# Cross attention's probabilities turned two steps behind, its last tiles added while it drains, and the query weight's low half made in parts on VectorE

## The chip, the cores and the metric

The kernel runs on one core of a Trainium2 chip. The metric is the device time of one execution in microseconds (us). A core has five engines that work beside each other and meet only in semaphores: TensorE (PE in the profile; PEld is its loading of weights), VectorE (DVE), ScalarE (ACT), GpSimd (POOL) and SyncE (SP), which here only issues transfers from device memory. Each engine takes its instructions strictly in the order in which they are written: an instruction that waits holds up all that stand behind it on its engine.

## What is computed

One block of a transformer on 32 sequences of 32 tokens, 512 wide, all in float32:

```python
x = x + xattn(layernorm(x), ctx, ctx)   # 16 heads of 32; ctx is (32, 257, 512)
x = x + attn(layernorm(x))              # self attention, four projections 512x512
x = x + ffn(layernorm(x))               # shared SwiGLU + 64 experts, top 8, 1536 wide

def xattn(q, k, v):                     # heads split from the 512 columns, no projections
    scores = einsum('bhqd,bhkd->bhqk', q, k) / sqrt(32)
    return einsum('bhqk,bhkd->bhqd', softmax(scores), v)
```

## The kernel before

The program has four stages, one behind the other, each a block in which the five engines run their own lists: cross attention (tiles named `a_...`, to about 201 us), self attention (`b_...`, to 353 us), the router with the shared network (`d_...`, to about 600 us) and the 64 experts (`e_...`, the rest). The 1024 tokens lie in eight tiles X of 128 x 512. Each of the first three stages begins with a layer norm of all eight tiles on VectorE (`layernorm`, line 81), with one square root on ScalarE in it.

**Cross attention** goes over 32 batches of 32 queries and 257 keys. A step of the loop does, for batch b:

- `scores(b)` on TensorE (line 250): four matmuls, one for four heads each, into PSUM banks 0 to 3. The queries of four heads stand as a block diagonal in `Q` (128 x 128), which GpSimd copies from XT (line 235). Before it, TensorE waits for K of batch b (`k_in`) and for the exponentials of batch b-1, which read the same banks.
- the largest score of each row on VectorE (`largest`, lines 336 and 340, in two halves), the exponential on ScalarE (line 316) into `PR`, and the division by the sum on VectorE (`normalise`, lines 346 and 348).
- `turn` on TensorE (lines 262 and 263): the normalised PR is transposed into banks 4 to 6. ScalarE copies two parts of it to `PTa` (line 310), VectorE the third to `PTb` (line 356).
- `values` on TensorE (line 281): 48 small matmuls with V into bank 7, which `place_out` on VectorE (line 329) copies to `AT`.

TensorE's list of step b is scores(b), values(b-3), turn(b-1). K and V have four buffers each. SyncE's list, which issues all of their copies, is

```python
for b in range(B):
    i = b % 4
    if b >= 4:
        sp.wait_ge(s_done, 2 * (b - 3))
    sp.dma_start(K[:, i, :, :], ctx_k[b])            # line 206
    if b >= 4:
        sp.wait_ge(pv_done, b - 3)
    sp.dma_start(V[0:KC, i, 0:2, :], ...)            # line 209
    sp.dma_start(V[0:KR, i, 2, :], ...)              # line 210
```

Here `s_done` counts finished halves of scores and `pv_done` finished `values`. V of batch b therefore waits for values(b-4), which frees its buffer, and K of batch b+1 stands behind V of batch b in the same list. After the last V come the four projection weights `W` of the next stage.

Once the loop has ended, the eight tiles of AT are transposed back (line 298), added to X (line 367), and the sums for the next layer norm are taken (`tile_stats`, line 76).

**Self attention** splits each float32 operand into a high half (ScalarE) and a low half, the remainder (VectorE), and multiplies three times. Its start: layer norm of eight tiles; ScalarE makes the high half of the query weight (line 567); GpSimd makes its low half (line 436) and clears `PT` (line 437); TensorE transposes four tiles in two banks (line 447), ScalarE copies them (line 591), VectorE finds masked tokens (line 622) and makes the low halves (line 624); then TensorE projects queries and keys of the first four tiles (lines 453 to 455), transposes the other four, and projects those. ScalarE takes the queries (line 581), VectorE the keys (line 637).

**The router's stage** begins in the same way, and GpSimd fills the masks and number tables for it (lines 1111 to 1119) as soon as the stage begins.

Of the kernel before, what the change touches and what calls it, by code (L numbers as in the profile page):

```python
# [10 lines left out]
ALU = mybir.AluOpType  # L11
# [69 lines left out]
def layernorm(dve, X, XN, mv, small, done, std_ready, xn_ready):  # L81
# [9 lines left out]
    for t in range(TT):  # L91
        dve.tensor_scalar(XN[:, t, :], X[:, t, :], mv[:, t, 0:1], r[:, t:t + 1],
                          ALU.subtract, ALU.mult).then_inc(xn_ready, 1)
# [22 lines left out]
def program(nc, x, ctx_k, ctx_v, wq, wk, wv, wo, bq, bk, bv, bo, wg, shared, experts, out):  # L116
    root = ExitStack()
    with root:
# [19 lines left out]
        narrow = sb("narrow", [1, NE], I32)  # L138
        x_dram = x.rearrange("b s d -> (b s) d").rearrange("(t p) d -> p t d", p=P)
# [11 lines left out]
        with ExitStack() as st:  # L151
# [3 lines left out]
            Q = sb("a_Q", [P, 4, G, P])  # L155
            K = sb("a_K", [P, 4, G, SK])
            V = sb("a_V", [P, 4, 3, D])
            PR = sb("a_PR", [P, 2, G, SK])
# [19 lines left out]
            zeroed = sem("a_zeroed")  # L178
            ident_ready = sem("a_ident_ready")
            q_ready = sem("a_q_ready")  # L180
# [12 lines left out]
            x1_ready = sem("a_x1_ready")  # L193

# [24 lines left out]
            def _(pool):  # L219
                pool.memset(ident[:, :], 0.0).then_inc(made, 1)  # L220
                pool.memset(Q[:, :, :, :], 0.0).then_inc(zeroed, 1)
# [3 lines left out]
                pool.wait_ge(zeroed, 1)  # L225

                for b in range(B):
                    i = b % 4
                    if i == 0:
                        pool.wait_ge(xt_copied, b // 4 + 1)  # L230
                    if b >= 4:
                        pool.wait_ge(s_done, 2 * (b - 3))
                    for h in range(4):
                        r = slice(32 * h, 32 * h + 32)
                        pool.tensor_copy(Q[r, i, :, r], XT[r, :, SQ * b:SQ * (b + 1)]).then_inc(q_ready, 1)

            @block.tensor
            def _(pe):
# [3 lines left out]

                def scores(b):
                    i = b % 4
                    pe.wait_ge(q_ready, 4 * b + 4)
                    pe.wait_ge(k_in[i], 16 * (b // 4) + 16)
                    for g in range(G):
                        if b >= 1:
                            pe.wait_ge(exp_done, 4 * (b - 1) + g + 1)
                        last = pe.matmul(ps[:, g, 0:SK], Q[:, i, g, :], K[:, i, g, :], start=True, stop=True)  # L250
                        if g % 2 == 1:
                            last.then_inc(s_done, 1)

                def turn(b):
# [5 lines left out]
                    for g in range(G):  # L260
                        for k in range(2):
                            pe.transpose(ps[0:KC, 4 + k, g * P:(g + 1) * P], PR[:, b % 2, g, k * KC:(k + 1) * KC], ident[:, :])
# [1452 lines left out]
```

## Time and profile before

| | |
|---|---|
| time, median of 3 runs | 2543.09 us (2541.92 to 2548.95) |
| the profiled execution: its time, its span | 2544.21 us, 2542.5 us |
| cross attention, to the end of its last sums | 200.9 us |
| self attention | 201.4 to 352.9 us |
| TensorE busy over the span | 2435.0 us (96%) |
| busy in one step of cross attention of 4.80 us | PE 4.27, DVE 3.91, ACT 3.00, POOL 2.04 us |

How to read it: the span runs from the first to the last instruction of the one profiled execution; its time is 1.7 us longer. From about 600 us on TensorE is busy practically all the time, and the change touches nothing there. What the change can move lies in the first 400 us, where the engines wait for each other. The granted clock of TensorE is written as a share of 2.4 GHz, so that 0.50 is 1.2 GHz.

### The profile page before, as it was taken

The numbers are of one execution on the slowest core, as the hardware profiler recorded it, in microseconds if no ns is written. First come the engines' busy times: TensorE is split into PE (matmuls) and PEld (weight loads), VectorE is DVE, ScalarE is ACT, GpSimd is POOL, SyncE is SP. The second block draws the span as 40 slices with busy tenths as digits, with TensorE's granted clock in tenths as the row PEclk, the third lists the DMA queues.
The fourth block names the chain that finished last, engine by engine and source line by source line (L and its number), as shares of the span: only waits on it lengthen the run. The fifth ranks groups of instructions, "written<-read, shape, count | busy, mean of one in ns | idle before, by whom it ended". The sixth has DMA issues, their size and how long they took to land.

```text
span 2542.5 us, 53551 instructions
## 1 busy us (share of the span) xinstructions
PE 2435.0 (96%) x22042; PEld 1994.8 (78%) x22042; DVE 1995.0 (78%) x1896; ACT 1690.0 (66%) x2119; POOL 639.5 (25%) x542
## 2 busy tenths in 40 slices
PE   6876989998999999999999999999999999999998
PEld 5765767776888888888888888888888888888886
DVE  6866557665799889998978988988778777767795
ACT  5642333334688778887867887877667767766784
POOL 3411010001132332332222233223222222222221
PEclk9987989998999999999999999999999999999999
DMA  6870022244899999998979999999888888887894
GB/s 201 224 221 0 2 106 110 86 161 166 300 378 381 362 344 384 375 374 332 375 288 326 367 355 351 385 356 344 303 296 325 327 300 325 326 296 280 311 372 133
DMA packets 128526, 714.99 MB, mean 281 GB/s; under 512 B 15488, under 2 KB 23808, under 8 KB 52416
## 3 DMA queue, kind: packets, MB, share of 16 engines
q1 hardware_dynamic: 102048, 665.96, 67.9%
q0 software_dynamic: 26144, 44.06, 8.3%
q8 instruction: 273, 4.47, 0.7%
q14 instruction: 61, 0.50, 0.1%
HBM read 684.46 MB, written 25.49 MB: 279 GB/s over the span
## 4 chain that ended last, share of the span: by engine, by line
PE 75%; issue 0%; DVE 0%; POOL 0%; ACT 0%; ACTq 0%; POOLq 0%; DVEq 0%
PE ps L1539 14%; PE ps L1541 14%; PE ps L1540 14%; PE ps L1617 7%; PE ps L1619 7%; PE ps L1618 7%; PE ps L1570 5%; PE ps L1589 4%; PE ps L1602 3%; PE ps L1527 1%; PE ps L1580 1%; PE ps L1530 0%; DVE e_WL L1430 0%; ACT e_WH L1348 0%; POOL out_rows L1501 0%
## 5 line engine op out<-in xcount | busy, mean ns | idle before, releaser
L1430 DVE TENSOR_TENSOR e_WL<-ring,e_WH 128x2048 fp32r<-128x2048 f32 x462 | 1057.3, 2289 | 234.0 <-ACT e_WH L1348 228.7
L1348 ACT ACTIVATE e_WH<-ring 128x2048 fp32r<-128x2048 f32 x462 | 885.1, 1916 | 125.1 <-PE ps L1541 56.9
L1539 PE MATMUL ps<-e_WH,e_XEh 128*128 128x512 f32 x1536 | 605.1, 394 | 3.6 <-DVE e_XEl L1452 3.6
L1541 PE MATMUL ps<-e_WH,e_XEl 128*128 128x512 f32 x1536 | 599.4, 390 | 0.0
L1540 PE MATMUL ps<-e_WL,e_XEh 128*128 128x512 f32 x1536 | 598.8, 390 | 0.0
L1489 POOL TENSOR_TENSOR e_tick<-e_tick 128x1 f32<-128x1 f32 x126 | 111.9, 888 | 1305.2 <-ACT X L1396 1184.6
L1539 PEld LDWEIGHTS ps<-e_WH,e_XEh 128*128 128x128 f32 x1536 | 289.0, 188 | 62.0 <-DVE e_XEl L1452 4.0
L1541 PEld LDWEIGHTS ps<-e_WH,e_XEl 128*128 128x128 f32 x1536 | 288.9, 188 | 61.2
L1540 PEld LDWEIGHTS ps<-e_WL,e_XEh 128*128 128x128 f32 x1536 | 289.1, 188 | 58.0
L1617 PE MATMUL ps<-e_WH,e_GTh 128*128 128x512 f32 x768 | 318.8, 415 | 0.0
L1430 DVE TENSOR_TENSOR e_WL<-e_more,e_WH 128x2048 fp32r<-128x2048 f32 x114 | 260.8, 2289 | 53.8 <-ACT e_WH L1348 52.5
L1619 PE MATMUL ps<-e_WH,e_GTl 128*128 128x512 f32 x768 | 301.7, 393 | 0.0
L1618 PE MATMUL ps<-e_WL,e_GTh 128*128 128x512 f32 x768 | 299.3, 390 | 1.1 <-issue 1.1
L1348 ACT ACTIVATE e_WH<-e_more 128x2048 fp32r<-128x2048 f32 x114 | 218.5, 1916 | 27.5 <-PE ps L1541 14.3
L1503 POOL DMA_INDIRECT out_rows<-X,lists x64 | 174.4, 2726 | 19.5 <-issue 19.5
L1619 PEld LDWEIGHTS ps<-e_WH,e_GTl 128*128 128x128 f32 x768 | 144.1, 188 | 33.9
L1618 PEld LDWEIGHTS ps<-e_WL,e_GTh 128*128 128x128 f32 x768 | 145.1, 189 | 26.4 <-issue 1.4
L1617 PEld LDWEIGHTS ps<-e_WH,e_GTh 128*128 128x128 f32 x768 | 144.5, 188 | 23.8 <-issue 0.4
L1356 ACT ACTIVATE X<-ps 128x512 f32<-128x512 f32 x192 | 115.3, 601 | 62.8 <-PE ps L1541 62.8
L1438 DVE TENSOR_TENSOR X<-X,ps 128x512 f32<-128x512 f32 x192 | 130.6, 680 | 4.0 <-PE ps L1541 4.0
L744 POOL DMA_INDIRECT XO<-xn_scratch,lists x64 | 127.1, 1986 | 19.5 <-issue 18.6
L1458 DVE TENSOR_TENSOR e_GTl<-ps,e_GTh 128x512 fp32r<-128x512 f32 x192 | 131.1, 683 | 0.0
(224 smaller groups left out, 3314.6 us busy)
## 6 DMA issues: line engine op xcount, KB each, us to landing
ring<-in_experts SPq DMA_DIRECT2D x462, 1024.0 KB, 8.3
e_more<-in_experts SPq DMA_DIRECT2D x114, 1024.0 KB, 8.4
ring<-in_shared SPq DMA_DIRECT2D x12, 1536.0 KB, 6.5
a_K<-in_ctx_k SPq DMA_DIRECT2D x32, 514.0 KB, 5.4
a_V<-in_ctx_v SPq DMA_DIRECT2D x32, 384.0 KB
a_V<-in_ctx_v SPq DMA_DIRECT2D x32, 130.0 KB
X<-in_x SPq DMA_DIRECT2D x4, 512.0 KB, 4.9
xn_scratch<-ring SPq DMA_DIRECT2D x1, 2048.0 KB, 7.4
```

What stands on the lines that cost most here:

```text
L1348: act.activation(WH[:, nth % HELD, :], unit(i), ACT.Copy).then_inc(hi_done, 1)
L1430: dve.tensor_tensor(WL[:, at, :], unit(place(kind, n)), WH[:, at, :], ALU.subtract).then_inc(lo_done, 1)
L1438: dve.tensor_tensor(GF[n % 2], SL[n % 2], up_ps, ALU.mult).then_inc(gf_done, 1)
L1458: dve.tensor_tensor(GTl[:, n % 2, :, :], turn_ps.rearrange("p (j n) -> p j n", j=G), GTh[:, n % 2, :, :], ALU.subtract).then_inc(gtl_done, 1)
L1503: pool.indirect_dma_start(out4, bass.IndirectOffsetOnAxis(lists[:, 1, e, 1:2], 0), Y2, None, compute_op=ALU.add).then_inc(added, 16)
L1539: pe.matmul(dst, h, wh, start=(k == 0), stop=False)
L1540: pe.matmul(dst, h, wl, start=False, stop=False)
L1541: last = pe.matmul(dst, l, wh, start=False, stop=(k == G - 1))
L1570: pe.matmul(over_ps[32 * c:32 * c + 32, kind * P:(kind + 1) * P], XEo[:, e % 2, k, :], w[:, k * D + c * P:k * D + (c + 1) * P], start=(kin ...
L1617: pe.matmul(down_ps, h, wh, start=(b == 0 and j == 0), stop=False)
L1618: pe.matmul(down_ps, h, wl, start=False, stop=False)
L1619: last = pe.matmul(down_ps, l, wh, start=False, stop=(b == NB - 1 and j == G - 1))
```

## The change

Five parts.

1. *Scores without the block diagonal.* `Q` and GpSimd's copies are gone. `scores` multiplies the 32 rows of each head from XT with K, four matmuls of 32 x 32 x 257 for each of four groups; the result of head h of group g lands in output rows 32*((g+h) mod 4), and `values` reads it from there.
2. *Turned two steps behind.* TensorE's step is now scores(b), values(b-4), turn(b-2). PR has three buffers. ScalarE and VectorE copy the turned parts three steps behind, and VectorE does both halves of `largest` before `normalise`. SyncE's list is unchanged.
3. *The last tiles are added in the drain.* Each of the steps 32 to 35 also transposes two tiles back, adds them and takes their sums.
4. *GpSimd idle during layer norms.* In self attention the clearing of PT waits until the first queries are taken; in the router's stage the masks and tables wait until all eight normalised tiles are written. After the last work of ScalarE in the first two stages, a square root into an unused tile is added, which leaves the table for square roots loaded.
5. *Start of self attention.* The query weight's low half is made in four column parts on VectorE, the first behind four tiles of the layer norm, the others behind the other four. Four PSUM banks instead of two hold transposed tiles, and the masks of four tiles are found by one instruction. TensorE transposes tiles 4 to 7 between the query and the key projection of the first half.

The core of the diff:

```diff
@@ scores, on TensorE @@
-                        last = pe.matmul(ps[:, g, 0:SK], Q[:, i, g, :], K[:, i, g, :], start=True, stop=True)
+                        for h in range(4):
+                            r = slice(32 * h, 32 * h + 32)
+                            last = pe.matmul(ps[column(g, h), g, 0:SK], XT[r, g, at], K[r, i, g, :], start=True, stop=True,
+                                             skip_group_check=True)
@@ the loop on TensorE @@
-                for b in range(B + 3):
+                for b in range(B + 4):
                     if b < B:
                         scores(b)
-                    if b >= 3:
-                        values(b - 3)
-                    if 1 <= b <= B:
-                        turn(b - 1)
+                    if b >= 4:
+                        values(b - 4)
+                    if 2 <= b <= B + 1:
+                        turn(b - 2)
+                    for t in tiles_back(b):
+                        turn_back(t)
@@ the loop on VectorE @@
+                for b in range(B + 4):
+                    if 3 <= b < B + 3:
+                        copy_rest(b - 3)
                     if b < B:
                         largest(b, 0)
+                        largest(b, 1)
                     if 1 <= b <= B:
                         normalise(b - 1)
-                    if b < B:
-                        largest(b, 1)
-                    if b >= 3:
-                        place_out(b - 3)
+                    if b >= 4:
+                        place_out(b - 4)
+                    for t in tiles_back(b):
+                        add_attended(t)
@@ self attention, GpSimd @@
-                pool.wait_ge(wh_done, 1)
-                pool.tensor_tensor(pair(QUERY)[1], whole(QUERY), pair(QUERY)[0], ALU.subtract).then_inc(wl_pool, 1)
+                pool.wait_ge(q_copied, 1)
                 pool.memset(PT[:, :, :, :, :], 0.0).then_inc(zeroed, 1)
@@ end of ScalarE's list in cross attention; the same in self attention @@
+                act.activation(unused[:, :], ident[:, 0:1], ACT.Sqrt)
@@ router's stage, GpSimd @@
+                pool.wait_ge(xn_ready, TT)
                 pool.memset(before[:, :], 1.0).then_inc(masks, 1)
```

**TensorE, one step in the middle of cross attention.** `a_k_in0` is the arrival of K in buffer 0, `a_v_in1` that of V in buffer 1, and so on; the order of the kernel before:

```order
L250 MATMUL ps<-a_K,a_Q 128x257 [waits a_exp_done,a_k_in0,a_q_ready]
L250 MATMUL ps<-a_K,a_Q 128x257 [waits a_exp_done] x3
L281 MATMUL ps<-a_PTa,a_V 32x32 [waits a_v_in1,a_at_ready,a_ptb_ready,a_pta_ready]
L281 MATMUL ps<-a_PTa,a_V 32x32 x7
L281 MATMUL ps<-a_PTb,a_V 32x32 x4
...
L262 MATMUL ps<-ident,a_PR 96x128 [waits a_ptb_ready,a_pta_ready,a_pr_ready]
L262 MATMUL ps<-ident,a_PR 96x128
```

and of the changed kernel:

```order
L253 MATMUL ps<-a_K,a_XT 32x257 [waits a_exp_done,a_k_in1]
L253 MATMUL ps<-a_K,a_XT 32x257 x3
L253 MATMUL ps<-a_K,a_XT 32x257 [waits a_exp_done]
...
L286 MATMUL ps<-a_PTa,a_V 32x32 [waits a_v_in1,a_at_ready,a_ptb_ready,a_pta_ready]
L286 MATMUL ps<-a_PTa,a_V 32x32 x7
L286 MATMUL ps<-a_PTb,a_V 32x32 x4
...
L266 MATMUL ps<-ident,a_PR 96x128 [waits a_ptb_ready,a_pta_ready,a_pr_ready]
L266 MATMUL ps<-ident,a_PR 96x128
```

The wait for GpSimd's copies (`a_q_ready`) is gone, scores are sixteen matmuls, and the values that stand behind the scores of buffer n are now those of buffer n itself (the batch four steps back) and no longer those of buffer n+1.

**VectorE, the end of cross attention**, from the last division of scores on, before (of eight additions two are shown):

```order
L348 TENSOR_TENSOR a_PR<-a_PR,a_rs 128x1028
L329 COPY a_AT<-ps 128x4x32
L356 COPY a_PTb<-ps 65x512
L329 COPY a_AT<-ps 128x4x32 x2
L367 TENSOR_TENSOR X<-X,ps 128x512
L76 BN_STATS stats<-X 128x6
L78 BN_AGGR mv<-stats 128x2
```

and now:

```order
L363 TENSOR_TENSOR a_PR<-a_PR,a_rs 128x1028
L344 COPY a_AT<-ps 128x4x32
L369 TENSOR_TENSOR X<-X,ps 128x512
L76 BN_STATS stats<-X 128x6
L78 BN_AGGR mv<-stats 128x2
...
L377 COPY a_PTb<-ps 65x512
L344 COPY a_AT<-ps 128x4x32
```

The additions stand between the copies of the last steps and no longer behind all of them.

**VectorE, the start of self attention**, before:

```order
L90 TENSOR_TENSOR small<-small 128x8
L92 TENSOR_SCALAR b_XN<-X,mv,small 128x512 x8
L622 TENSOR_SCALAR b_mask<-ps 1x128
L624 TENSOR_TENSOR b_XTl<-ps,b_XTh 128x512
...
L630 TENSOR_TENSOR b_WP<-W,b_WP 128x2048
L679 TENSOR_TENSOR X<-X,bvo 128x512 x8
L637 TENSOR_SCALAR b_KT<-ps,bqk 128x512 x4
```

and now:

```order
L97 TENSOR_TENSOR small<-small 128x8
L84 TENSOR_SCALAR b_XN<-X,mv,small 128x512 x4
L659 TENSOR_TENSOR b_WP<-W,b_WP 128x4x128
L647 TENSOR_TENSOR b_XTl<-ps,b_XTh 128x512 x4
L652 TENSOR_SCALAR b_mask<-ps 1x512
L84 TENSOR_SCALAR b_XN<-X,mv,small 128x512 x4
L659 TENSOR_TENSOR b_WP<-W,b_WP 128x4x128 x3
L664 TENSOR_TENSOR b_WP<-W,b_WP 128x2048
L718 TENSOR_TENSOR X<-X,bvo 128x512 x8
```

Half of the layer norm has moved behind what the first projection waits for, and the quarter of the query weight's low half that it needs first has moved ahead of the transposed tokens.

## Rows read from the trace of the kernel before

**Rows 1.** Windows: length; busy time (instructions) of each engine; PEclk; DMA share; GB/s.

```profile
35.60:35.90 0.30, 0.30 (x40) 0.23 (x26) 0.30 (x1) 0.30 (x2) 0.30 (x1) 1.00 0.00 0
...
100.00:104.80 4.80, 4.27 (x118) 3.56 (x117) 3.91 (x8) 3.00 (x11) 2.04 (x4) 1.00 0.85 218
...
175.00:180.00 5.00, 4.22 (x109) 3.75 (x112) 0.78 (x2) 0.49 (x1) 0.00 (x0) 0.52 1.01 406
```

**Rows 2.** Timeline, PE, one step: start, length, line, names, count [idle before].

```profile
99.94 1.91 PE L250 MATMUL ps<-a_K,a_Q 128*128 128x257 f32 x8
101.78 0.33 PE L281 MATMUL ps<-a_PTa,a_V 96*32 96x32 f32 x16
...
103.33 0.42 PE L262 MATMUL ps<-ident,a_PR 128*96 128x128 f32 x2 [0.53 <-DVE a_PR L348]
...
104.58 0.27 PE L263 MATMUL ps<-ident,a_PR 128*65 128x128 f32 x1
```

**Rows 3.** Timeline, SyncE, in the same step: issue of V.

```profile
102.84 0.31 SPq L209 DMA_DIRECT2D a_V<-in_ctx_v  x1
```

**Rows 4.** Timeline: issue of a later K on SyncE, and the scores that use it.

```profile
127.82 1.44 SPq L206 DMA_DIRECT2D a_K<-in_ctx_k  x1
...
133.96 1.98 PE L250 MATMUL ps<-a_K,a_Q 128*128 128x257 f32 x8 [0.17 <-issue]
```

**Rows 5.** DMA issues, landing in us: the K issued at 127.82, then that at 36.80.

```profile
a_K<-in_ctx_k SPq DMA_DIRECT2D x1, 514.0 KB, 6.1
...
a_K<-in_ctx_k SPq DMA_DIRECT2D x1, 514.0 KB, 5.5
```

**Rows 6.** Tile a_K, all 32 copies: time from issue to landing.

```profile
DMA to landing us min/median/max: 3.5/5.4/13.7
```

**Rows 7.** Timeline, SyncE: V of batch 4, then K of batch 5.

```profile
35.97 0.31 SPq L209 DMA_DIRECT2D a_V<-in_ctx_v  x1
...
36.80 0.35 SPq L206 DMA_DIRECT2D a_K<-in_ctx_k  x1
```

**Rows 8.** Timeline, PE, in the drain: after a pause, and a whole turn.

```profile
175.78 0.27 PE L281 MATMUL ps<-a_PTb,a_V 65*32 65x32 f32 x3 [2.67 <-issue]
...
176.68 0.66 PE L262 MATMUL ps<-ident,a_PR 128*96 128x128 f32 x2
...
179.05 0.42 PE L263 MATMUL ps<-ident,a_PR 128*65 128x128 f32 x1
```

**Rows 9.** Timeline, PE, at the start of self attention's projections.

```profile
220.01 0.76 PE L453 MATMUL ps<-b_XTh,b_WP 128*128 128x512 f32 x1 [1.69 <-DVE b_XTl L624]
...
223.09 0.39 PE L454 MATMUL ps<-b_XTl,b_WP 128*128 128x512 f32 x1
```

**Rows 10.** Timeline: V of batch 31 on SyncE; VectorE's last sums of cross attention.

```profile
165.85 0.31 SPq L209 DMA_DIRECT2D a_V<-in_ctx_v  x1
...
200.74 0.18 DVE L78 BATCH_NORM_AGGREGATE mv<-stats 128x2 f32<-128x6 f32 x1
```

**Rows 11.** Timeline: eight tiles normalised (first, second layer norm); two of them turned, PE.

```profile
12.47 3.74 DVE L92 TENSOR_SCALAR a_XN<-X,mv,small 128x512 f32<-128x512 f32 x8
...
204.07 11.37 DVE L92 TENSOR_SCALAR b_XN<-X,mv,small 128x512 f32<-128x512 f32 x8
...
204.67 1.97 PE L447 MATMUL ps<-ident,b_XN 128*128 128x128 f32 x8 [6.55 <-DVE b_XN L92]
```

**Rows 12.** Timeline: last keys of the first half, first queries of the second.

```profile
243.51 0.75 DVE L637 TENSOR_SCALAR b_KT<-ps,bqk 128x512 f32<-128x512 f32 x1 [1.97 <-PE ps L455]
...
251.69 0.69 ACT L581 ACTIVATE b_QT<-ps,bqk 128x512 f32<-128x512 f32 x1 [4.04 <-PE ps L455]
```

**Rows 13.** Timeline, third layer norm: a 128x8 operation on VectorE; ScalarE behind a transfer.

```profile
355.13 4.17 DVE L89 TENSOR_SCALAR small<-small 128x8 f32<-128x8 f32 x1
...
360.27 1.06 ACT L890 ACTIVATE d_UPh<-ring 128x1024 fp32r<-128x1024 f32 x1 [5.88 <-DMA ring<-in_shared]
```

**Rows 14.** Timeline, PE, self attention: scores of one tile in 32 x 32 pieces.

```profile
319.88 1.29 PE L506 MATMUL ps<-b_KT,b_QT 32*32 32x32 f32 x128
```

More of the change, by code:

```diff
@@ L78, in tile_stats, with layernorm_tiles, layernorm @@
     dve.bn_aggr(mv[:, t, :], stats[:, t, :]).then_inc(stats_done, 1)
-def layernorm(dve, X, XN, mv, small, done, std_ready, xn_ready):
+def layernorm_tiles(dve, X, XN, mv, small, xn_ready, first, end):
+    for t in range(first, end):
+        dve.tensor_scalar(XN[:, t, :], X[:, t, :], mv[:, t, 0:1], small[:, 1, t:t + 1],
+                          ALU.subtract, ALU.mult).then_inc(xn_ready, 1)
+def layernorm(dve, X, XN, mv, small, done, std_ready, xn_ready, first=0, end=TT):
     var, r, a = small[:, 0, :], small[:, 1, :], small[:, 2, :]
@@ L90, in layernorm @@
     done.then(dve.tensor_tensor(r, r, a, ALU.mult))
-    for t in range(TT):
-        dve.tensor_scalar(XN[:, t, :], X[:, t, :], mv[:, t, 0:1], r[:, t:t + 1],
-                          ALU.subtract, ALU.mult).then_inc(xn_ready, 1)
+    layernorm_tiles(dve, X, XN, mv, small, xn_ready, first, end)
 def transpose_tiles(pe, ps, XN, ident, xn_ready, xt_psum, xt_copied):
@@ L543, in project_out @@
                     last.then_inc(o_psum, 1)
-                for half in range(2):
-                    for t in range(4 * half, 4 * half + 4):
-                        turn_tile(t)
-                    project(QUERY, half)
-                    project(KEY, half)
+                for t in range(4):
+                    turn_tile(t)
+                project(QUERY, 0)
+                for t in range(4, TT):
+                    turn_tile(t)
+                project(KEY, 0)
+                project(QUERY, 1)
+                project(KEY, 1)
                 for t in range(TT + 3):
@@ L672, in add_out @@
                     tile_stats(dve, X, stats, mv, t, o_added, t + 1, stats2)
-                layernorm(dve, X, XN, mv, small, Tally(dve, ln_done), std_ready, xn_ready)
+                layernorm(dve, X, XN, mv, small, Tally(dve, ln_done), std_ready, xn_ready, 0, 4)
+                query_weights_low(0)
                 for t in range(4):
                     tokens_low(t)
+                find_masked(0)
+                layernorm_tiles(dve, X, XN, mv, small, xn_ready, 4, TT)
+                for o in range(1, G):
+                    query_weights_low(o)
                 weights_low(KEY)
```

133 lines of the change are left out of this document (68 added, 65 removed).

## The prediction

> **What bounds the kernel now.** I read four views, in this order. The windows by stage show that the engines share the work only in the first 400 us, and that one step of cross attention lasts 4.80 us with TensorE busy for 4.27 and VectorE for 3.91 of it [rows 1]: no engine is full, so a chain through several engines or a transfer sets the step. The timeline of TensorE shows one such chain: scores at 99.94, values at 101.78, then 0.53 us of waiting for VectorE's division, the turn from 103.33 to 104.85, and the next scores at once [rows 2]. The change goes for this chain, and the 0.53 us are what it can win in a step.
>
> The timeline of SyncE together with the landings shows a second chain, just as long. V of a batch goes out the moment values(b-4) is done (102.84) [rows 3], and K of the next batch behind it. The K issued at 127.82 takes 6.1 us and lands at 133.92; its scores begin at 133.96, after TensorE has stood idle for 0.17 us, which the profile files under issue because it shows no transfer there [rows 4, 5]. So in the kernel before K is already only just in time, with a whole step plus a turn of lead.
>
> **Part by part. The queue that the values are moved past.** In the changed kernel values(b-4) is done in step b, not in step b-1. SyncE's list is as before: V(b) waits for it, and K(b+1) waits in the list behind V(b), though its own buffer has long been free. Step b+1 begins with scores(b+1), which need this K. Of the lead (a turn and a whole step) only the turn is left, 1.5 us [rows 2]. The loop is now closed within one step: K landed, scores, values, V issued, K issued, K landed. Its terms:
>
> - scores and values at full clock: from 99.94 to the issue of V at 102.84, 2.90 us [rows 2, 3].
> - from V's issue to K's landing: V of batch 4 goes out at 35.97 and K of batch 5 at 36.80, into a DMA queue that had nothing to do just before (share 0.00), which is how it will be in every step of the changed kernel. K lands 5.5 us later, 6.33 us after V's issue [rows 1, 5, 7]. In the worst place it was 0.83 + 6.1 = 6.9. A K of 3.5 us, the shortest of all 32, is the bound on the other side: 4.3 [rows 6]. I take 6.33, the case that is alike.
>
> That is a step of 9.23 us in place of 4.81 at full clock, with TensorE idle for 6.33 - 1.52 = 4.8 us in each.
>
> **The clock.** In the drain of the kernel before, TensorE paused for 2.67 us up to 175.78 and went on at a granted clock of 0.52, which is its lower level of 1.2 GHz [rows 1, 8]. A turn then took from 176.68 to 179.47, 2.79 us, against 1.52 at 2.4 GHz, a factor of 1.84 [rows 2, 8]. It came back to full clock 3.1 us after the projections had begun at 220.01 (a matmul of 512 columns goes from 0.76 to 0.39 us) [rows 9]. With a pause longer than 2.67 us in every step, each step's scores should begin at the low level. If scores and values all run there they take 2.90 x 1.84 = 5.34 us and the step 11.67; if the clock returns after 3.1 us, these do 1.7 us of the work and the remaining 1.2 us run at full clock: 4.3, and a step of 10.6. I take the middle, 11.1, since nothing in the rows decides it. The Trainium skill describes this very loop (TensorE: Matmul & The Clock Gate, "HAM oscillation"): matmuls, then a wait for a transfer, and every round starts throttled again; by it every step pays. The trace agrees for one pause, at 175.78; no run here shows a repeated one.
>
> **The scores themselves.** 16 matmuls of 32 x 32 in place of 4 of 128 x 128: each of the 8 passes of 257 columns takes about 0.23 us (1.91 / 8), and there are now 32 passes. If the four heads' pieces run at the same time the cost is nothing; if in pairs, 1.9 us more; if one by one, 5.5 more [rows 2]. In self attention 128 passes of 32 columns in such pieces take 1.29 us [rows 14]; one by one they would take 128 x 0.23 x 32/257 = 3.7. I take nothing. The Trainium skill (TensorEngine Tiling (Array Packing), "Gotcha 1: PSUM Pressure") speaks against this form: pieces in different row groups cannot write one PSUM bank at the same time, and here all four do. By that rule they would run one by one; the row at 319.88, also four row groups in one bank, is nearly three times faster than that, so I give the rule a small chance.
>
> The copies on GpSimd (2.04 us per step [rows 1]) cost nothing before and win nothing now.
>
> **Sum of the loop.** V(4) goes out after values(0), in step 4 instead of 3, but the steps before it are shorter, since their K is there: it stays near 36 (2 us either way). Then 27 steps of 11.1: V(31) at 335.7 in place of 165.85 [rows 10], **+169.8 us**.
>
> **The drain.** From V(31) to the end of the last sums it was 200.92 - 165.85 = 35.1 us [rows 10]. Now VectorE does the eight additions with their sums (1.52 us each, 12.2 in all: they fill 188.67 to 200.92 today) between the copies, and its own work in the four last steps, with one division and seven copies, comes to 18 us. Two waits for TensorE and pauses like the 2.67 us [rows 8] stay: I take 24, **-11** (from -14 to -5).
>
> **Start of self attention.** Eight tiles take 11.37 us while GpSimd works, and 3.74 while it doesn't, 0.47 each [rows 11]. The stage begins at 201.4. Its small operations take 2.65 us before the first tile at 204.07 and without the table load 1.3 less; so the first tile is there after 1.35 + 0.47 + some 0.3 of semaphores = 2.1 us. TensorE turns two tiles in 1.97 us at the low clock [rows 11], four in 4: 6.1. ScalarE's copy and VectorE's low half of the last one, 0.6 and 0.7, end at 7.5. VectorE meanwhile has four tiles (1.9) and a quarter of the weight (0.7) done. I put the first projection at 7.7 us; it was 18.6 (220.01) [rows 9]: **-10.9**. Between the halves: from the last keys (PE done near 243.5) to the second half's first queries at 251.69, less the 2.7 us that a group takes, lie 5.5 us [rows 12]; four tiles turned in a row at full clock cost 2: **-3.5**. GpSimd's clearing of PT now falls on the key weight's low half; that has 5 us of slack behind the second set of turns.
>
> **Third layer norm.** One operation on 128x8 elements took 4.17 us beside GpSimd [rows 13]; its neighbours of the same size take 0.17. Without that and the table load the layer norm is 5.4 us shorter. But ScalarE can copy nothing before 361.33, since it waits for the first weights, issued when the stage begins [rows 13]: the gain stops there, **-0.3**.
>
> Total: 169.8 - 11 - 10.9 - 3.5 - 0.3 = +144. The span becomes 2686.5 us, the profiled execution, 1.7 us longer than its span, 2688, and the median of the runs, 1.1 us under it, **2687 us**.
>
> **The rivals.**
> 1. *The clock holds.* The loop as above, but with 9.23 us in a step: 27 x 1.87 = 50 us less, and 2.5 less in the drain: 2634. For it: the work of a step is 4.4 us, longer than the 3.1 that brought the clock back. Against it: the pause.
> 2. *Scores in pairs or one by one.* In pairs +1.9 (3.5 at low clock) in each of 27 steps gives 2740 to 2780; one by one 2835 to 2960.
> 3. *Faster: K arrives in time.* If the copies no longer queue behind a backlog, the landing after V's issue could shrink. The step would fall to TensorE's 4.27 us [rows 1] only if K landed 1.5 us after V's issue; then 27 x 0.54 = 15, 11 and 15 us are won: 2502. All parts together break even where a step lasts 5.8 us, a landing 2.9 us after V's issue. The quickest case that the rows allow is 4.3, a step of 7.2 and 2579 us; that mechanism wins nothing either.
> 4. *The change does not do what it says*: a step keeps 4.8 us since another wait (exponentials) takes over; then only the 26 us at the ends are won, 2517. It needs K in time as well.
>
> **Chances.** Forecast (low clock in most steps) 0.65; rival 1, 0.20; rival 2, 0.06 in pairs and 0.03 one by one; rivals 3 and 4 together 0.05; 0.01 for exactly no change. The range goes from 2620, a full clock with landings of 5.8 us, to 2745, a step at the low clock throughout with landings of 6.9 us and some loss in the scores. A measurement can tell about 0.3% (7.6 us) from no change; faster 0.05, same 0.01, slower 0.94.
>
> **What would show it.** SyncE's V should follow each other every 11 us from V(4) on, each K landing 0.05 us before its scores; TensorE's idle time before the scores (filed under issue) should be 27 times 3 to 5 us, and its clock between 20 and 330 us clearly under 1. The wait of the turn for the division should be gone. Self attention's first projection should start under 9 us after the stage begins. It is wrong if V's spacing is 5 us or less (K was no bound), or 9.3 with a clock of 1.00.

## The result, and the profile after

| | before | after |
|---|---|---|
| median of 6 runs | 2543.14 us (2541.92 to 2548.95) | 2622.11 us (2612.85 to 2624.2) |
| ratio after / before | | 1.030 (95% interval 1.0285 to 1.032) |
| profiled span | 2542.5 us | 2621.4 us |

The changed kernel is 79 us slower. The forecast was 144 us slower: the direction was right, and so was the loop that was to cause it; one price in it was wrong.

The page of the changed kernel: the clock granted to TensorE in 40 slices, then the group of the scores (busy us, mean ns of one, and idle time before them with what ended it).

```profile
span 2621.4 us, 54951 instructions
...
PEclk8666898999899999999999999999999999999999
...
L253 PE MATMUL ps<-a_K,a_XT 32*32 32x257 f32 x1024 | 37.9, 558 | 103.4 <-DMA a_K<-in_ctx_k 100.3
```

The first slices, which hold cross attention, have a low clock, and TensorE has waited 100.3 us for K. The view of waits between 40 and 270 us has one row for it (total, times, longest):

```profile
PE ps L253 <- DMA a_K<-in_ctx_k: 100.3, 27, 6.0
```

One step, from the timeline of all engines (start, length, engine, line, names, count, idle time before):

```profile
122.42 0.31 SPq L216 DMA_DIRECT2D a_V<-in_ctx_v  x1
...
123.24 0.35 SPq L213 DMA_DIRECT2D a_K<-in_ctx_k  x1
...
128.97 1.17 PE L253 MATMUL ps<-a_K,a_XT 32*32 32x257 f32 x32 [4.78 <-DMA a_K<-in_ctx_k]
...
131.51 0.66 PE L266 MATMUL ps<-ident,a_PR 128*96 128x128 f32 x2
...
131.64 0.31 SPq L216 DMA_DIRECT2D a_V<-in_ctx_v  x1
```

This is the closed loop that the prediction drew: V goes out after values(b-4), K behind it in SyncE's list, the next scores at the moment this K lands, and values and V behind these. The turn begins at 131.51 without any wait, so the 0.53 us of [rows 2] are indeed gone. TensorE stood idle for 4.78 us instead.

SyncE's timeline, V of batch 4 and V of batch 31:

```profile
35.36 0.31 SPq L216 DMA_DIRECT2D a_V<-in_ctx_v  x1
...
270.04 0.31 SPq L216 DMA_DIRECT2D a_V<-in_ctx_v  x1
```

27 steps in 234.68 us are 8.69 us each, where the kernel before had 4.81 [rows 7, 10] and the prediction 11.1. V of batch 31 goes out 104.2 us later than in [rows 10].

The windows (length, busy time and instructions of each engine, clock, DMA share, GB/s) show how low the clock was over the loop:

```profile
40.00:100.00 60.00, 35.65 (x980) 26.94 (x980) 26.18 (x56) 19.82 (x63) 0.00 (x0) 0.60 0.40 117
100.00:150.00 50.00, 28.16 (x834) 21.61 (x835) 22.12 (x47) 17.31 (x53) 0.00 (x0) 0.70 0.43 121
```

From 200 to 250 us it is 0.64. A mean of 0.6 to 0.7 is a mix of 1.2 and 2.4 GHz: in the step shown the scores and values run at the low level, and the turn goes over to the full one. In 22 of the 27 steps the scores take 1.17 us, as here; in three they take 0.73 us, at the full level, and in two 0.91.

Behind the loop: VectorE's last sums of cross attention; TensorE at the start of self attention and, at 313.58, turning four tiles between the halves; VectorE's last keys of the first half; ScalarE's first queries of the second half, and its first work on weights in the stage of the third layer norm:

```profile
294.39 0.18 DVE L78 BATCH_NORM_AGGREGATE mv<-stats 128x2 f32<-128x6 f32 x1
```

```profile
302.27 0.50 PE L475 MATMUL ps<-b_XTh,b_WP 128*128 128x512 f32 x1 [1.42 <-DVE b_XTl L647]
...
313.58 1.91 PE L469 MATMUL ps<-ident,b_XN 128*128 128x128 f32 x16
```

```profile
326.44 0.75 DVE L671 TENSOR_SCALAR b_KT<-ps,bqk 128x512 f32<-128x512 f32 x1 [1.97 <-PE ps L477]
```

```profile
329.16 0.69 ACT L605 ACTIVATE b_QT<-ps,bqk 128x512 f32<-128x512 f32 x1 [12.74 <-PE ps L477]
...
437.82 1.06 ACT L930 ACTIVATE d_UPh<-ring 128x1024 fp32r<-128x1024 f32 x1 [6.71 <-DMA ring<-in_shared]
```

How the 78.9 us between the two spans add up:

| stretch | before | after | difference | forecast |
|---|---|---|---|---|
| to V of batch 31 | 165.85 | 270.04 | +104.2 | +169.8 |
| from there to the end of the last sums | 35.1 | 24.5 | -10.5 | -11 |
| from there to the first projection | 19.1 | 7.7 | -11.4 | -10.9 |
| from there to the second half's first queries | 31.7 | 26.9 | -4.8 | -3.5 |
| from there to ScalarE's first work on weights in the router's stage | 108.6 | 108.7 | +0.1 | -0.3 |
| from there to the end | 2182.2 | 2183.6 | +1.4 | 0 |
| sum | | | +78.9 | +144 |

Of the 4.8 us, 3.6 are the ones that the prediction meant: from the last keys to the second half's first queries it was 8.2 us, 5.5 more than a group takes, and is now 2.7, with 1.9 us for the turns ahead of it. The third layer norm wins nothing, since ScalarE still starts behind a transfer (437.82), as in [rows 13]. Every line but the first is within 1.4 us of its forecast. So the question for the experiments is the first one: why 8.69 us and not 11.1, and whether the loop through SyncE's list really is the cause.

### The profile page after: what moved, and what is told of

Read it like the earlier page. It is cut to its first block, busy times and chain, and to the rows that moved or that the text cites. A ratio compares the mean times of both kernels' runs of the same rounds, so it can differ in the third digit from the quotient of the medians.

```text
span 2621.4 us, 54951 instructions
## 1 busy us (share of the span) xinstructions
PE 2446.3 (93%) x22810; PEld 1990.8 (76%) x22810; DVE 1983.8 (76%) x1894; ACT 1689.9 (64%) x2121; POOL 571.5 (22%) x412
## 4 chain that ended last, share of the span: by engine, by line
PE 73%; issue 0%; DVE 0%; POOL 0%; ACT 0%; ACTq 0%; POOLq 0%; DVEq 0%
PE ps L1580 13%; PE ps L1582 13%; PE ps L1581 13%; PE ps L1658 7%; PE ps L1660 7%; PE ps L1659 7%; PE ps L1611 5%; PE ps L1630 3%; PE ps L1643 3%; PE ps L1568 1%; PE ps L1621 1%; PE ps L1571 0%; DVE e_WL L1471 0%; ACT e_WH L1389 0%; POOL out_rows L1542 0%
## 5 line engine op out<-in xcount | busy, mean ns | idle before, releaser
L329 ACT ACTIVATE a_PR<-ps,a_nm 128x257 f32<-128x257 f32 x128 | 59.1, 474 | 131.0 <-DVE a_nm L355 131.0
L253 PE MATMUL ps<-a_K,a_XT 32*32 32x257 f32 x1024 | 37.9, 558 | 103.4 <-DMA a_K<-in_ctx_k 100.3
```

## The experiments

Each run is given with its ratio to the kernel before, which ran on the same chip beside it (its median was 2543 to 2545 us each time).

**Where the missing 2.4 us of a step are: the price of the scores.** In the step shown above, 32 passes of 257 columns took 1.17 us at the low level of the clock, less than 8 whole passes at the full one (1.91 us, [rows 2]). The prediction had taken the old price, 1.91 at full and 3.5 at the low level. The first theory was that the order of the pieces makes the difference: with `(g + h) % 4` the four heads of four column groups land in sixteen different pieces of the array, which can all work at once; with the heads on the diagonal only four can.

```diff
                 def column(g, h):
-                    c = (g + h) % 4
+                    c = h
                     return slice(32 * c, 32 * c + 32)
```

> The changed kernel with one thing undone: the scores of head h land in output rows 32*h in every group (and the values read them there), so the sixteen matmuls of a step use four 32x32 pieces of the array four times each, not sixteen pieces once each. Theory (the step was shorter than forecast since sixteen pieces run at the same time): the 32 passes fall from 1.2 us to about 3.4 us at the low clock (four at a time, 0.43 us each), they lie on the loop through the K copy, and the step grows from 8.7 to 10.5 to 11 us: 27 steps, 2622 + 50 to 60 = 2670 to 2685 us. Rival (the pieces' positions do not matter, the forecast was only wrong on clock and landing): 2622 us, step 8.7.

Measured: 2680.0 us (2678.67 to 2680.96), ratio 1.053 (1.0514 to 1.0549). TensorE in one step, then V of batches 4 and 31:

```profile
119.77 3.31 PE L253 MATMUL ps<-a_K,a_XT 32*32 32x257 f32 x32 [5.07 <-DMA a_K<-in_ctx_k]
```

```profile
35.94 0.31 SPq L216 DMA_DIRECT2D a_V<-in_ctx_v  x1
...
328.68 0.31 SPq L216 DMA_DIRECT2D a_V<-in_ctx_v  x1
```

The same 32 passes now take 3.31 us, the last part of them at the full clock (the granted clock is 0.57 from 119.77 to 123.08); where the clock is 0.50 throughout, as from 97.43 on, they take 3.65. A step takes (328.68 - 35.94) / 27 = 10.84 us. In the first steps of this kernel, at full clock, the scores take 1.94 us, the price of the whole ones (1.91). With the price of scores that the prediction assumed, the kernel does what the prediction said: 10.84 against 11.1, 2680 against 2687. The rival, that the order of the pieces is of no account, falls. One line is worth 58 us here, since in a closed loop every microsecond of work counts.

**Whether SyncE's list is the cause.** K goes into the list two batches ahead of V; nothing else is altered.

```diff
-                for b in range(B):
-                    i = b % 4
-                    if b >= 4:
-                        sp.wait_ge(s_done, 2 * (b - 3))
-                    sp.dma_start(K[:, i, :, :], ctx_k[b]).then_inc(k_in[i], 16)
-                    if b >= 4:
-                        sp.wait_ge(pv_done, b - 3)
-                    ...  # V of batch b
+                for b in range(B + 2):
+                    if b < B:
+                        if b >= 4:
+                            sp.wait_ge(s_done, 2 * (b - 3))
+                        sp.dma_start(K[:, b % 4, :, :], ctx_k[b]).then_inc(k_in[b % 4], 16)
+                    v = b - 2
+                    if v >= 0:
+                        if v >= 4:
+                            sp.wait_ge(pv_done, v - 3)
+                        ...  # V of batch v
```

> The changed kernel with SyncE's list alone reordered: K of batch b+2 is issued before V of batch b, all waits as they were. Theory (K behind V in the list closes the loop within one step): TensorE no longer waits for K (100 us of waits gone), the step falls from 8.7 us to what VectorE (4.1) or TensorE (3.5 to 4) needs, 4.1 to 4.4 us, clock near 1.00: 2622 - 27*4.4 = 2500 to 2512 us. Rival (the copies themselves are too slow or the two-step lag itself costs a wait): the step stays over 6 us and the time over 2550.

Measured: 2519.11 us (2517.99 to 2519.7), ratio 0.990 (0.9883 to 0.9916). The time falls by 103 us: the whole loss of 79 us is gone, and the kernel is 1% faster than before. V of batch 31, then TensorE's waits between 35.5 and 165 us (in total, times, longest), then a window:

```profile
167.75 0.31 SPq L218 DMA_DIRECT2D a_V<-in_ctx_v  x1
```

```profile
PE ps L288 <- issue: 12.7, 13, 2.0
PE ps L255 <- issue: 6.0, 5, 2.4
PE ps L268 <- issue: 4.3, 2, 3.0
PE ps L269 <- issue: 3.0, 1, 3.0
```

```profile
100.00:160.00 60.00, 48.87 (x1769) 36.95 (x1760) 47.35 (x103) 36.93 (x116) 0.00 (x0) 0.88 0.81 221
```

No wait for K is left. But the time is 7 us above what was expected, and the loop is no faster than before (V of batch 31 at 167.75, against 165.85 in [rows 10]): 26.0 us of pauses filed under issue have come in, which the kernel before does not have there. They are taken up below.

With K one batch ahead (the same edit with 1 for 2):

> The changed kernel with K of batch b+1 issued before V of batch b (one ahead and not two). Theory (the loop then spans two steps: 6.0 us from V's issue to K's landing and 1.9 to 2 us of scores and values in two steps, 4.0 us each): hardly different from two ahead, 4.1 to 4.5 us per step, 2500 to 2515 us. Rival (K must be two steps ahead to be in time): steps of 5 us and more.

Measured: 2520.65 us (2519.26 to 2524.07), ratio 0.991 (0.9888 to 0.9928). TensorE's waits from 35.5 to 165 us:

```profile
PE ps L255 <- DMA a_K<-in_ctx_k: 18.1, 17, 2.3
```

K is late again in 17 steps, by 1.1 us on average, and yet the time is the same within the intervals: there are fewer pauses filed under issue, 14.4 us in all in place of 26.0, so that the waits for K seem to lie where pauses would have been. One batch of lead nearly does it, a second one removes the wait.

The same edit on the kernel before asks whether K was a bound there, where it had a step and a turn of lead:

> The kernel before with the same reordering of SyncE's list alone. Theory (in the kernel before both chains are nearly equal: the steps of 4.9 to 5.2 us are waits for K, the others the chain through the division, 4.75): mean step from 4.81 to 4.73 us, 2541 us, a gain of 1 to 3 us. Rival (K alone sets the step of the kernel before): the step falls to TensorE's 4.3, 2530 us or less.

Measured: 2541.29 us (2539.12 to 2545.49), ratio 0.999 (0.9977 to 0.9996). K was just in time before, as [rows 4] suggested, but it cost little: the interval is 0.04 to 0.23%, 1 to 6 us. It is the lag that made it one.

**The parts at the ends alone.** Cross attention as before (with its table load for the square root moved, as in the changed kernel), and the changed start of self attention, its halves and the layer norms.

> Cross attention as before, with only the added square root at its end; self attention and the router's stage as in the changed kernel (parts 4 and 5 alone). Theory: the terms of the forecast for the starts of the stages hold by themselves, -11 (first projection), -3.5 (between the halves), -0.3 (third layer norm): 2528 us. Rival (they hid behind the stretched cross attention, or the port and clock differ): 2535 to 2543.

Measured: 2529.49 us (2529.07 to 2531.32), ratio 0.994 (0.9925 to 0.9958). TensorE's first projection in its timeline:

```profile
210.53 0.79 PE L461 MATMUL ps<-b_XTh,b_WP 128*128 128x512 f32 x1 [1.41 <-DVE b_XTl L633]
```

The span fell by 15.1 us, against -10.9 - 3.5 - 0.3 = -14.7 in the prediction. Beside it one sees what the new cross attention wins once K is in time: the kernel with K two ahead has its V of batch 31 at the same place (167.75; 167.89 here), and its first projection at 200.14, 10.4 us earlier. All of its gain is in the drain.

**What the clock costs.** 14 transposes of the identity into a free part of a bank fill a part of TensorE's wait for K.

```diff
                         turn(b - 2)
+                    if 4 <= b < B - 1:
+                        pe.wait_ge(exp_done, 4 * b + 1)
+                        for _ in range(14):
+                            pe.transpose(ps[:, 0, 3 * P:4 * P], ident[:, :], ident[:, :])
```

> The changed kernel with fourteen transposes of the unit matrix added at the end of TensorE's steps 4 to 30, into unused columns of bank 0, once this batch's first exponential is done; nothing reads them. About 3.1 us at full clock, in the time in which TensorE waits for K. Theory (the low clock lengthens scores and values within the loop): the granted clock of cross attention rises from 0.6 to 0.7 to 0.9 or more, the stretch from scores to V's issue falls from 2.7 to 1.9 to 2.1 us, the step from 8.7 to 8.0: 2600 to 2607 us. Rival (the clock costs nothing here, the loop is copies): 2622; if the transposes reach into the next scores: above 2622.

Measured: 2604.33 us (2599.42 to 2604.79), ratio 1.023 (1.0209 to 1.0252), 17.8 us under the changed kernel. TensorE and, of the same stretch, the window:

```profile
128.37 1.86 PE L310 MATMUL ps<-ident 128*128 128x128 f32 x14
...
132.18 0.73 PE L253 MATMUL ps<-a_K,a_XT 32*32 32x257 f32 x32 [1.95 <-DMA a_K<-in_ctx_k]
```

```profile
100.00:160.00 60.00, 43.24 (x1219) 36.67 (x1220) 29.58 (x63) 22.25 (x71) 0.00 (x0) 0.86 0.46 130
```

With a wait of 1.95 us in place of 4.78, the scores begin at the full clock and take 0.73 us. V goes out at 133.93, 1.75 us behind the scores; in the changed kernel it was 2.67 (131.64 - 128.97). A step fell from 8.69 to 8.10 us ((255.23 - 36.47) / 27). Over the 27 steps, scores and values took 2.60 us on average in the changed kernel and 1.95 here, while the stretch from V's issue to the next scores stayed at 6.1. So the low clock was a cost, but not the main one: these 18 us of the 79, and some 23 by an estimate in which every step has 1.75 us in place of 2.60 (0.86 was granted here, not 1.00). The rest is the wait for K.

**The lags of before with the small scores.** Values three batches and the turn one batch behind, as before; all else as in the changed kernel.

```diff
                     if b < B:
                         scores(b)
-                    if b >= 4:
-                        values(b - 4)
-                    if 2 <= b <= B + 1:
-                        turn(b - 2)
+                    if b >= 3:
+                        values(b - 3)
+                    if 1 <= b <= B:
+                        turn(b - 1)
```

> The changed kernel with the order of the kernel before in its loop (values three steps behind, turn one, the copies two, the division between the halves of the largest), all else kept: scores in sixteen pieces, tiles added in the drain, starts of the stages. Theory (the queue of K costs only through the moved values): K has a whole step and a turn again, 6.3 + 2 us in two steps allows 4.2; the chain scores, largest, division, turn loses 0.5 us of scores: step 4.3 to 4.6, total 2502 to 2514 us. Rival (something else of the change makes K late): step over 6, above 2550.

Measured: 2529.77 us (2527.87 to 2535.65), ratio 0.994 (0.9922 to 0.9958), over 15 us more than expected. (Its profile is of the slowest of its four executions, 2535.65 us.) And with K two ahead as well:

> The same with K issued two batches ahead of V as well. Theory: if K was what held the kernel before it at 4.3 to 4.6, the step falls a little further to the chain's 4.2 to 4.4; 0 to 5 us faster than without. It shows whether two steps of lag are worth anything once K is in time: the two-step kernel with keys ahead should be at VectorE's 4.1 to 4.2, 3 to 8 us faster than this one.

Measured: 2526.89 us (2521.15 to 2530.28), ratio 0.994 (0.9916 to 0.9956); its profile is of the fastest execution. TensorE's waits from 35.5 to 165 us, first without K ahead, then with it:

```profile
PE ps L266 <- DVE a_PR L363: 21.8, 20, 1.3
PE ps L286 <- issue: 11.1, 4, 5.0
PE ps L253 <- DMA a_K<-in_ctx_k: 4.1, 3, 2.1
PE ps L266 <- issue: 1.4, 1, 1.4
PE ps L267 <- issue: 0.7, 1, 0.7
PE ps L253 <- issue: 0.7, 2, 0.4
```

```profile
PE ps L268 <- DVE a_PR L365: 21.0, 22, 1.3
PE ps L288 <- issue: 8.2, 5, 2.5
PE ps L255 <- issue: 1.8, 3, 0.8
PE ps L269 <- issue: 1.3, 1, 1.3
PE ps L268 <- issue: 1.1, 1, 1.1
```

Two things are seen. With the lag of before, K is nearly in time without any help (4.1 us): putting back the lag alone removes 92 of the 103 us. And the wait for the division is now 21 us, since the shorter scores leave less to cover it; the second step of lag takes it away entirely (there is no such row with K two ahead), but 26.0 us of pauses stand there, where these two kernels have 13.9 and 12.4. Of the 21 us that the lag saves, 7.8 are left in the time (2526.89 against 2519.11), at the upper end of what was expected.

**What the pauses are.** One of them in the kernel of the next experiment, in TensorE's timeline:

```profile
76.36 0.27 PE L300 MATMUL ps<-a_PTa,a_V 96*32 96x32 f32 x8
81.12 0.28 PE L300 MATMUL ps<-a_PTa,a_V 96*32 96x32 f32 x3 [4.50 <-issue]
```

It lies inside the 96 multiplications of one values(b), where no wait stands. The pages of all kernels list a queue that carries instructions (q8), and the view of DMA shows its packets in time (packets, MB, share of 16 engines). From 68.6 to 78.5 us only data moves; then from 78.5 to 78.6:

```profile
q1 hardware_dynamic: 843, 2.07, 97.6%
```

```profile
q8 instruction: 1, 0.02, 72.2%
```

For 10 us, with the DMA engines busy with K and V for 97.6% of the time, no packet of instructions comes. The one that begins at 78.55 has 16 KB and lands at 79.71, and TensorE goes on 1.4 us later, at 81.12. This is no accident of one pause. Between 35.5 and 175 us the traces of all kernels here have 57 pauses of over 0.9 us filed under issue, and 56 of them end 1.2 to 1.7 us after such a packet has landed, while these packets never come less than 3.3 us apart. The pause of 2.67 us in the drain of the kernel before [rows 8] is one more: a packet lands at 174.53, and TensorE goes on at 175.78. So TensorE waits there for its own instructions.

Three kernels were made to find what sets these pauses. The first puts back the whole scores, from the tile that GpSimd fills. In the profile's count a step then has 116 multiplications (8 for the scores, 96 for the values, 12 for the turn) in place of 140.

```diff
-                        for h in range(4):
-                            r = slice(32 * h, 32 * h + 32)
-                            last = pe.matmul(ps[column(g, h), g, 0:SK], XT[r, g, at], K[r, i, g, :], start=True, stop=True,
-                                             skip_group_check=True)
+                        last = pe.matmul(ps[:, g, 0:SK], Q[:, i, g, :], K[:, i, g, :], start=True, stop=True)
```

> The changed kernel with K two batches ahead of V in SyncE's list, and with the scores as in the kernel before: 4 matmuls (8 passes) of 128 x 128 from the tile that GpSimd fills, in place of 16 (32 passes) of 32 x 32. With small pieces this order took 2519.1 us, 12 more than expected, and its trace shows pauses of TensorE filed under issue, 0.9 to 3.2 us long, about every tenth step, which the kernel before has not in its loop (118 matmuls in 4.8 us there). Theory 'supply of instructions': the 24 more passes with 24 more weight loads per step are more than TensorE's list is refilled with beside a busy DMA; with 8 passes again the pauses over 0.9 us vanish from the loop, the clock stays at 1.00 in it, a step lasts what TensorE works, 4.3 to 4.5 us, V(31) goes out near 155 instead of 167.8, and the time is 2502 to 2511. Rival 'the two steps of lag': the pauses belong to the new order or to K ahead; they stay, and since whole scores take 1.2 us more than the small pieces, a step is 5.0 to 5.2 and the time 2520 to 2532.

Measured: 2518.78 us (2511.45 to 2520.11), ratio 0.989 (0.9869 to 0.9909). The waits from 35.5 to 165 us, and V of batch 31:

```profile
PE ps L300 <- issue: 11.0, 6, 4.5
PE ps L280 <- issue: 2.3, 1, 2.3
PE ps L268 <- issue: 1.1, 2, 0.8
```

```profile
171.40 0.31 SPq L221 DMA_DIRECT2D a_V<-in_ctx_v  x1
```

Neither theory holds as it was put. The pauses are 14.4 us in place of 26.0, with fewer instructions, but they don't go, and the longest is even longer (4.5). Without them a step is (171.40 - 36.03 - 14.4) / 27 = 4.48 us, against (167.75 - 35.45 - 26.0) / 27 = 3.94 with small scores. So small scores are worth 0.54 us in a step, 14.7 us in all, and 11.6 us more of pauses stand against it: the two nearly cancel, and the times are the same. That the 24 more multiplications are what brings these 11.6 us is likely but not shown: each kernel has one trace, and the one with the lags of before has 140 multiplications too and 12.4 us of pauses.

The second loads V for the first four batches only.

```diff
-                    if v >= 0:
-                        if v >= 4:
-                            sp.wait_ge(pv_done, v - 3)
+                    if 0 <= v < 4:
```

> The changed kernel with K two batches ahead, and V loaded for the first four batches alone (batches 4 to 31 use V of batch b mod 4: that part is left out, the work of the engines is the same). It takes half of the DMA traffic out of the loop. Theory 'refills stand behind data': TensorE's pauses filed under issue come from instruction refills that queue behind K and V; with half the traffic they shrink under 0.9 us or go, the clock stays near 1.00, a step is set by VectorE's 3.9 us, and the time is 2490 to 2503. Rival 'number alone': TensorE's list is refilled at its own pace whatever the traffic; the pauses stay and the time is 2513 to 2520.

Measured: 2508.19 us (2506.44 to 2509.58), ratio 0.986 (0.9838 to 0.9871), between the two theories. With V left out the attention values are others, so that 2508 is not quite the time of the same work. The third loads K too for the first four batches only:

> As the kernel without the traffic of V, and K too is loaded for the first four batches alone (batches 4 to 31 use K and V of batch b mod 4; the engines do the same work). No data moves during the loop. With half of the traffic TensorE's pauses filed under issue had added up to 27.0 us between 35.5 and 156 us, against 26.0 with all of it, so they had not shrunk. Theory 'own pace': TensorE's list of instructions is refilled no faster than this loop uses it up, whatever else moves; the pauses stay at 15 us or more, and the time is 2502 to 2510. Rival 'any data in front': K's transfers alone are enough to hold the refills up; without them the pauses fall under 5 us, the clock is 1.00 in the loop, a step takes 3.9 us, and the time is 2482 to 2495.

Measured: 2520.34 us (2519.46 to 2526.0), ratio 0.991 (0.9889 to 0.9924). That time can't be compared: with other attention values the tokens go to other experts, and TensorE has 23683 multiplications in place of 22810. The loop can. First TensorE's waits with V's traffic gone, from 35.5 to 156 us; then those without any traffic, from 35.5 to 150 us, with a window of the same kernel:

```profile
PE ps L286 <- issue: 21.6, 18, 3.2
PE ps L266 <- issue: 2.8, 2, 1.5
PE ps L253 <- issue: 2.6, 4, 1.7
```

```profile
PE ps L284 <- issue: 10.7, 18, 1.5
PE ps L264 <- issue: 3.1, 2, 1.8
PE ps L251 <- issue: 1.7, 4, 0.7
...
PE ps L265 <- issue: 1.1, 1, 1.1
```

```profile
100.00:160.00 60.00, 50.10 (x1962) 39.09 (x1963) 52.04 (x112) 39.33 (x114) 0.00 (x0) 0.97 0.02 5
```

With half of the traffic 27.0 us of pauses are left, as many as with all of it, and yet the kernel is 11 us faster: the last scores run at 160.6 us in place of 165.7, the first projection at 193.0 in place of 200.1. With none (share 0.02) 16.6 us are left, the longest 1.8 us in place of 3.0, and the last scores run at 144.9. So the larger part of the pauses doesn't come from data in the queues. TensorE uses up its instructions faster than they come, and data makes some of the pauses longer. Of the theories "own pace" is the nearer one, since the pauses stayed above its bound of 15 us. Traffic has a part of 9.4 us in the pauses, and of 21 us in the length of the loop; the other 11 us of that are not put down to anything by these runs, though the granted clock was higher too (0.97 against 0.88 from 100 to 160 us).

## Why the prediction was right or wrong

**What bounds the kernel: right.** The second chain, SyncE's list with K behind V, is what took over. Taking K out from behind V gives back 103 us of 2622, and restoring the lag alone gives back 92.

**V's issue to K's landing, 6.33 us: right.** From V's issue to the next scores it took 6.1 us on average over the 27 steps (5.4 to 7.7). Reading V and K of batches 4 and 5, which went into an empty queue [rows 1, 5, 7], was the right choice among 4.3, 6.33 and 6.9.

**The scores, "I take nothing": wrong, and this is nearly the whole miss.** The prediction asked only whether the small pieces are slower than the whole matmul, and bounded the price from above (in pairs, one by one). That they could be faster it did not consider. Scores and values took 2.67 us at the low clock, where 4.3 to 5.34 was reckoned, and 1.75 at full clock, where it was 2.90. The step is 11.1 - 8.69 = 2.4 us shorter than forecast; 27 of them are 65 us, all of the difference between 2687 and 2622. Of these, 58 are the scores' price, as the run with the pieces on the diagonal shows: there the price of the whole matmul returns (3.65 us at the low clock, 3.5 assumed; 1.94 at full clock), the step is 10.84 and the time 2680. The last 7 us are the landing, 6.1 in place of 6.33.

The rows on record could not have shown this gain. In self attention the pieces lie on the diagonal too (head h in row group h and column group h), and by the prediction's own figure its 128 passes in 1.29 us [rows 14] are 3.7 / 1.29, some three at a time. Only a row of pieces spread over all sixteen positions would have priced them.

**The rule on PSUM banks: it does not hold here.** Four row groups write one bank in the changed kernel. The 32 passes take 0.73 us at full clock, where one after another they would take 7.6 (32 x 0.24, from 1.91 / 8), so some ten are under way at a time; one piece at a time in each of the four banks would allow four. The Trainium skill (TensorEngine Tiling (Array Packing), "Gotcha 1: PSUM Pressure") says that different row tiles cannot access the same bank simultaneously; the measurement decides against it for this form, in which the pieces write different partitions of the bank. The chance for passes one by one (0.03, with 0.06 for pairs) was rightly small, but the lesson was on the other side.

**The clock: right in kind, half in size.** It is low in most steps, 0.60 to 0.70 over the loop, as forecast. The Trainium skill's picture of it (TensorE: Matmul & The Clock Gate, "HAM oscillation") is that each round begins slow after its wait; the trace agrees for 22 of the 27 steps (scores of 1.17 us), while in five the scores began at the full clock (0.73 and 0.91 us). But the low clock multiplies the work between two waits, and as that was smaller, the cost was too: 2.67 - 1.75 = 0.9 us in a step instead of 1.87. Filling a part of the wait won 18 us. The first rival, "the clock holds", gave 2634 and lies nearer to 2622 than the forecast, but for a wrong reason: the clock did not hold.

**The ends: right.** Drain 24.5 us (24 forecast), start of self attention 7.2 us from the stage's first operation (295.07) to the first projection (7.7), the halves -3.6 (-3.5). The third layer norm won nothing (-0.3). The run with the stage starts alone moved the span by -15.1 (-14.7).

**Rival 3, K in time: 2502 forecast.** It did not happen in the changed kernel, but K two ahead makes it, and gives 2519. What was missing in that sum are the pauses in which TensorE waits for its instructions. In the loop of the kernel before there were none of over 0.2 us; that its waits for the division left TensorE the time is the likeliest reason, but no run isolates it. The prediction had seen one in the drain [rows 8] and allowed for such pauses there, but not in a loop that would run without waits.

**The signs to look for.** V's spacing was to be 11 us and was 8.7; K's landing just ahead of its scores, 27 waits (3.7 us on average, 3 to 5 forecast, though filed under the transfer and not under issue), the low clock, the missing wait for the division and a first projection under 9 us were all there.

## What to carry to other kernels

When work is moved one step later, look at every queue whose entries wait for that work: what stands behind the waiting entry is moved too, and a lead of a step and a turn can shrink to a turn. In a loop closed through a transfer every operation counts in full, in both directions: before one takes an operation's price as unchanged, its new form has to be priced, also for a gain. And a loop with no waits left is not yet at its engines' busy time: with over a hundred small multiplications in a step, TensorE had to wait here for its own instructions, and that took back much of what the change had won. Such a pause has no releaser in the view of waits; laying the packets of the instruction queue beside it in time shows what ended it.

The best of the kernels here keep the changed kernel's order and put K two batches ahead of V: 2519 us, with small or with whole scores, 1% under the kernel before.

## What the runs showed of the hardware

- **Order of small pieces on TensorE.** 32 passes of 32 x 32 pieces with 257 columns took 1.17 us when four neighbouring multiplications in each of four groups covered all sixteen pieces, and 3.65 us when all groups used the four on the diagonal, both at the low clock. At the full clock it was 0.73 and 1.94 us, and 1.91 for the 8 whole 128 x 128 passes.
- **TensorE waits for its instructions.** Pauses of 0.5 to 5.0 us in the middle of multiplications without a wait, once the loop has few other waits; 56 of the 57 of over 0.9 us end 1.2 to 1.7 us after a packet of 16 KB has landed on the instruction queue. They are 26.0 us in 130 with 140 multiplications in a step, 14.4 us with 116, and none of over 0.2 us in the kernel before (one of 1.0 where its cross attention ran with the new ends), which also has 116 but waits 0.5 us in each step. Without data traffic 16.6 us, the longest 1.8. With them the clock falls too (0.83 to 0.88 in that loop, 1.00 before). Why a packet comes late stays open: the rate alone doesn't decide it, since the kernel with whole scores runs, its pauses included, fewer multiplications per us (116 in 5.01 us) than the kernel before (116 in 4.81). Data in the DMA queues is a part: the longest pause but one (4.5 us) followed 10 us without a packet, in which data kept the DMA engines 97.6% busy.
